# One chip core, three attention-like parts: layer-norm normalisations on ScalarE, and other slots for statistics, projections and fetches

## What is computed

```python
x = x + _layernorm(_L0_attn_ref(_layernorm(x), w_qkv, w_out, b_out))
x = x + _layernorm(_L0_ffn_ref(_layernorm(x), ...))
# _L0_ffn_ref:
for l in range(2):
    x = x + _attn(_ln(x, ln1_w[l], ln1_b[l]), wq[l], wk[l], wv[l], wo[l], ...)   # 16 heads of 8, causal
    h = _ln(x, ln2_w[l], ln2_b[l])
    moe = _token_moe if l % 2 == 0 else _seq_moe     # top 2 of 8 experts, per token / per sequence
    x = x + moe(h, ...)                              # experts 128 -> 512 -> 128, exact gelu
# _ln and _layernorm: (x - mean) / sqrt(var + 1e-5), the first with weight and bias
```

## Time and profile of the kernel before

| | |
|---|---|
| Median of 3 runs | 1273.79 us (1273.51 to 1277.96) |
| The profiled execution | 1271.35 us, of which the trace spans 1269.6 |
| Mean granted clock of TensorE | 0.943 |
| TensorE busy | 1064.3 us (84%) |
| VectorE busy | 936.9 us (74%) |
| ScalarE busy | 767.8 us (60%) |
| GpSimd busy | 663.6 us (52%) |

### The profile page before, as it was taken

How to read it: one execution, slowest core, us unless ns; L and a number is a source line. 1 busy time by engine, 2 the same in 40 slices (tenths; PEclk the granted TensorE clock), 3 DMA queues, 4 the chain that set the end, 5 groups by cost and what they waited for, 6 DMA issues and landing times. The chain is left out here.

```text
span 1269.6 us, 36493 instructions
## 1 busy us (share of the span) xinstructions
PE 1064.3 (84%) x10172; PEld 795.5 (63%) x10267; DVE 936.9 (74%) x2774; ACT 767.8 (60%) x1745; POOL 663.6 (52%) x986
## 2 busy tenths in 40 slices
PE   1888999999999899998199997387888989959997
PEld 0565666666666666665199997255655656638996
DVE  3678999999988889997523332278889888865665
ACT  1566777777777777776066564156657667645554
POOL 3345565566556777776611111566676666422332
PEclk8899999999999999999599999589989899988999
DMA  5332111111112122211222222243221211100000
GB/s 148 93 96 78 51 49 38 42 49 52 53 52 59 45 64 63 67 51 37 75 63 70 70 70 71 56 115 103 76 65 39 65 47 55 53 2 9 17 21 21
DMA packets 120793, 74.57 MB, mean 59 GB/s; under 512 B 7936, under 2 KB 115712, under 8 KB 120704
## 3 DMA queue, kind: packets, MB, share of 16 engines
q1 hardware_dynamic: 101536, 54.48, 15.5%
q10 hardware_dynamic: 15072, 10.61, 2.9%
q0 software_dynamic: 4096, 8.40, 2.2%
HBM read 22.21 MB, written 12.71 MB: 28 GB/s over the span
## 5 line engine op out<-in xcount | busy, mean ns | idle before, releaser
L608 DVE TENSOR_REDUCE negm<-bank 128x2 f32<-128x512 f32 (+1 forms) x576 | 389.1, 679 | 84.2 <-PE bank L300 59.0
L496 ACT ACTIVATE prob<-bank 128x512 f32<-128x512 f32 x576 | 339.7, 595 | 126.6 <-PE bank L322 88.5
L889 POOL TENSOR_SCALAR_AFFINE_SELECT prob<-prob 128x512 f32<-128x512 f32 x384 | 248.3, 648 | 171.3 <-ACT prob L496 169.1
L341 PE MATMUL bank<-prob,vaug 128*32 128x256 f32 (+1 forms) x3072 | 168.7, 338 | 1.6 <-POOL prob L889 1.3
L308 PE MATMUL bank<-stack 126*128 126x256 bf16 x768 | 152.3, 280 | 0.0
L327 PE MATMUL bank<-stack 128*128 128x256 bf16 x768 | 150.7, 278 | 0.9 <-ACT prob L496 0.9
L1180 POOL COPY w_job<-w_s 128x512 f32 x72 | 47.1, 655 | 191.7 <-PE bank L1150 183.0
L1161 PEld LDWEIGHTS bank<-w_job,prob 128*128 128x128 f32 x1152 | 139.6, 192 | 3.6
L1161 PE MATMUL bank<-w_job,prob 128*128 128x128 f32 x1152 | 139.9, 275 | 0.0
L341 PEld LDWEIGHTS bank<-prob,vaug 128*32 128x32 f32 x3072 | 81.6, 111 | 78.5 <-issue 46.7
L1172 ACT ACTIVATE prob<-bank,b_job 128x256 f32<-128x256 f32 x288 | 118.2, 469 | 16.4 <-PE bank L1150 15.1
(11 more groups left out here) (180 smaller groups left out, 2003.7 us busy)
## 6 DMA issues: line engine op xcount, KB each, us to landing
stack<-parts SPq DMA_DIRECT2D x288, 128.0 KB
w_s<-e_w ACTq DMA_DIRECT2D x32, 256.0 KB, 2.9
oT<-x_routed SPq DMA_DIRECT2D x40, 128.0 KB, 2.1
y_routed<-oT SPq DMA_DIRECT2D x40, 128.0 KB, 1.8
stack<-mT SPq DMA_DIRECT2D x192, 4.0 KB
out<-x_all SPq DMA_DIRECT2D x16, 128.0 KB, 1.8
b_all<-e_b ACTq DMA_DIRECT2D x2, 512.0 KB, 8.3
x_routed<-hk,x_at POOLq DMA_INDIRECT x64, 2.3
```

The costliest lines, as they stand in the source:

```text
L341: m = nc.tensor.matmul(o, w, (prob0, prob1)[kb][:, g % 2, h], start=kb == 0, stop=kb == 1, skip_group_check=True)
L496: nc.scalar.activation(o, s, ACT.Exp, scale=SCALE).then_inc(exp_done, 1)
L608: nc.vector.tensor_reduce(o, s, AX.X, ALU.max, negate=True).then_inc(max_done, 1)
L889: nc.gpsimd.affine_select(out=t, in_=t, compare_op=ALU.is_ge, fill=0.0, base=0, pattern=[[0, HG], [1, P]], channel_multiplier=-1).then_inc ...
```

## The change

The normalisation (x - mean) * r is written as x * r + c with c = -mean * r, so that ScalarE's activation can do it with scale and bias by partition. GpSimd computes c for both tiles of an item (`pool_shift`, two small operations) behind each `pool_rstd` of xn and of att/hn, always in slot 2. ScalarE writes xn in slot 3 (`act_xn`, behind the copy mT) and att or hn at the end of slot 2 (`act_post`). The normalisation `f` stays on VectorE.

Moved on VectorE: f from slot 0 to slot 1 (ahead of the reductions of that slot, and one more step behind: item first), the statistics and moments of the new x from slot 3 to slot 0 of the next step, the combine of phase 2 from slots 0 and 1 (item nxt2) to slots 2 and 3 of the step before (nxt3). On TensorE: `pe_o3` from slot 0's end to an early place in slot 1, `pe_v` from the end of slot 2 (item nxt) to the end of slot 1 (item cur, the step after); ScalarE's writes of v go from slot 3 to slot 2. On GpSimd: the power for f from slot 0 to slot 3, the fetches from one per slot to two in slot 3 (item 4 ahead) and two in slot 0 (item 3 ahead), always behind the slot's last select. The run of phase 2 begins one step sooner. The four writes of q and k keep their order: the fourth now stands at the start of slot 1 instead of the end of slot 0. Three semaphores are new (`post_n`, `x_rstd`, `f_ok`); what waited for `res` of the normalisations waits for these.

```diff
-NPRE, NRSTD, NRES, NSPLIT = 4, 4, 14, 3
+NPRE, NRSTD, NRES, NSPLIT = 4, 4, 10, 3
...
-            at = lo - (3 if hi == 3 * B else 2)
+            at = lo - (4 if hi == 3 * B else 2)
...
         def pe_hT(i):
-            pe.wait_ge(res, NRES * i.v + NRES)
+            pe.wait_ge(post_n, 2 * i.v + 2)
...
+            if k == 1 and older:
+                pe_o3(older)
...
             if im:
-                if gm == 0:
+                if gm == 1:
                     pe.wait_ge(v_sb, im.v + 1)
-                if gm == 2 and nxt:
-                    pe.wait_ge(v_sb, nxt.v + 1)
                 pe_max_T(im, gm)
...
-            if k == 0 and older:
-                pe_o3(older)
...
-            if k == 2 and nxt:
-                if im:
-                    pe.wait_ge(mT_sb, 4 * im.v + gm + 1)
-                pe_v(nxt)
+            if k == 1 and cur:
+                pe.wait_ge(mT_sb, 4 * cur.v + 1)
+                pe_v(cur)
...
+        def act_normal(dst, src, r, c, s):
+            for j in range(2):
+                nc.scalar.activation(dst[j], src[j], ACT.Identity, scale=r[:, j:j + 1],
+                                     bias=c[:, j:j + 1]).then_inc(s, 1)
+        def act_xn(i):
+            act.wait_ge(pre_rstd, NRSTD * i.v + NRSTD)
+            need(act, xT_ps, i.v - 1)
+            act_normal([xn[:, i.par, j] for j in range(2)], tiles(x_all if i.phase == 0 else f_all, i),
+                       pre_r[:, i.par], pre_c[:, i.par], xn_ok)
+        def act_post(i):
+            act.wait_ge(post_rstd, NRSTD * i.v + 4)
+            if i.phase == 0:
+                dst = src = [att[:, i.par, j] for j in range(2)]
+            else:
+                dst, src = [hn[:, i.par, j] for j in range(2)], tiles(f_all, i)
+                need(act, hT_ps, i.v - B - 1)
+                if i.phase == 1:
+                    need(act, hk_sb, i.v - B - 1)
+            act_normal(dst, src, post_r[:, i.par], post_c[:, i.par], post_n)
...
         def act_slot(step, k):
-            cur, nxt, nxt2, old, older = (item(step, d) for d in (0, 1, 2, -1, -2))
+            cur, nxt, nxt2, older = (item(step, d) for d in (0, 1, 2, -2))
             (ie, ge), (io, go), (im, gm) = group(step, k, 2), group(step, k, 4), group(step, k, 1)
-            if k == 3 and nxt:
-                act_values(nxt)
+            if k == 1 and nxt:
+                act_qk(nxt, 3)
+            if k == 2 and cur:
+                act_values(cur)
             if io:
                 act_oT(io, go)
             if ie:
                 act_exp(ie, ge, 0)
             if im:
                 act_mT(im, gm)
+            if k == 3 and nxt2:
+                act_xn(nxt2)
             if k == 0 and nxt:
                 act_qk(nxt, 0)
+                act_qk(nxt, 1)
...
+            if k == 2 and older:
+                act_post(older)
             if k == 0 and nxt:
-                act_qk(nxt, 1)
+                act_qk(nxt, 2)
...
-        def dve_normalise(i):
-            dve.wait_ge(post_rstd, NRSTD * i.v + (2 if i.phase == 0 else NRSTD))
-            if i.phase > 0:
-                need(dve, hT_ps, i.v - B - 1)
-                if i.phase == 1:
-                    need(dve, hk_sb, i.v - B - 1)
-                dve_normal([hn[:, i.par, j] for j in range(2)], tiles(f_all, i), post_mv[:, i.par],
-                           post_r[:, i.par], res, NRES - 7)
-            else:
-                att_j = [att[:, i.par, j] for j in range(2)]
-                dve_normal(att_j, att_j, post_mv[:, i.par], post_r[:, i.par], res)
...
         def dve_f(i):
-            dve.wait_ge(post_rstd, NRSTD * i.v + NRSTD)
-            dve_normal(tiles(f_all, i), tiles(x_all, i), mv2[:, i.par], r2[:, i.par], res)
+            dve.wait_ge(x_rstd, 2 * i.v + 2)
+            for j in range(2):
+                nc.vector.tensor_scalar(tiles(f_all, i)[j], tiles(x_all, i)[j], mv2[:, i.par, j, 0:1],
+                                        r2[:, i.par, j:j + 1], ALU.subtract, ALU.mult).then_inc(f_ok, 1)
...
+            if k == 1 and first and first.phase == 0:
+                dve_f(first)
...
-            if k == 3 and nxt2:
-                dve.wait_ge(pre_rstd, 2 * nxt2.v + 2)
-                need(dve, xT_ps, nxt2.v - 1)
-                dve_normal([xn[:, nxt2.par, j] for j in range(2)], tiles(x_all if nxt2.phase == 0 else f_all, nxt2),
-                           pre_mv[:, nxt2.par], pre_r[:, nxt2.par], xn_ok)
...
-            if k == 0 and nxt2 and nxt2.phase == 2:
-                dve_combine(nxt2, 0)
             if k == 0 and oldest and oldest.phase == 0:
-                dve_f(oldest)
+                dve_stats(tiles(x_all, oldest), st2, res, NRES * oldest.v + 6)
...
-            if k == 3 and older and older.phase == 0:
-                dve_stats(tiles(x_all, older), st2, res, NRES * older.v + 8)
+            if k == 3 and nxt3:
+                dve_combine(nxt3, 1)
...
-            if k == 1 and nxt2 and nxt2.phase == 2:
-                dve_combine(nxt2, 1)
-            if k == 2 and older:
-                dve_normalise(older)
+            if k == 0 and oldest and oldest.phase == 0:
+                need(dve, x_rstd, 2 * (oldest.v - 2) + 2)
+                dve_moments(st2, mv2[:, oldest.par], res, NRES * oldest.v + 6)
+            if k == 2 and nxt3:
+                dve_combine(nxt3, 0)
...
-            if k == 3 and older and older.phase == 0:
-                need(dve, post_rstd, NRSTD * (older.v - 2) + 4)
-                dve_moments(st2, mv2[:, older.par], res, NRES * older.v + 8)
...
+        def pool_shift(mv, r, c, s, base, last=1):
+            pool.wait_ge(s, base)
+            alone(pool)
+            for j in range(2):
+                nc.gpsimd.tensor_scalar(c[:, j:j + 1], mv[:, j, 0:1], r[:, j:j + 1], -1.0, ALU.mult,
+                                        ALU.mult).then_inc(s, last if j else 1)
...
-                pool_rstd(post_mv[:, older.par], post_r[:, older.par], post_rstd, NRSTD * older.v,
-                          1 if older.phase == 0 else NRSTD - 1)
-            if k == 0 and oldest and oldest.phase == 0:
-                pool.wait_ge(res, NRES * oldest.v + 12)
-                pool_rstd(mv2[:, oldest.par], r2[:, oldest.par], post_rstd, NRSTD * oldest.v + 2)
+                need(pool, post_n, 2 * (older.v - 2) + 2)
+                pool_rstd(post_mv[:, older.par], post_r[:, older.par], post_rstd, NRSTD * older.v)
+                pool_shift(post_mv[:, older.par], post_r[:, older.par], post_c[:, older.par], post_rstd,
+                           NRSTD * older.v + 2)
...
             if ie:
                 pool_select(ie, ge, 0)
+            if k == 3 and oldest and oldest.phase == 0:
+                pool.wait_ge(res, NRES * oldest.v + NRES)
+                need(pool, f_ok, 2 * (oldest.v - 2) + 2)
+                pool_rstd(mv2[:, oldest.par], r2[:, oldest.par], x_rstd, 2 * oldest.v)
...
-                pool_rstd(pre_mv[:, nxt2.par], pre_r[:, nxt2.par], pre_rstd, 2 * nxt2.v)
+                pool_rstd(pre_mv[:, nxt2.par], pre_r[:, nxt2.par], pre_rstd, NRSTD * nxt2.v)
+                pool_shift(pre_mv[:, nxt2.par], pre_r[:, nxt2.par], pre_c[:, nxt2.par], pre_rstd,
+                           NRSTD * nxt2.v + 2)
...
-            nxt3 = item(step, 3) if step_phase(step) == 2 else None
-            if nxt3:
-                pool_fetch(nxt3, k)
+            if step_phase(step) == 2 and k in (0, 3):
+                fetched_item = item(step, 4 if k == 3 else 3)
+                for n in range(2):
+                    if fetched_item:
+                        pool_fetch(fetched_item, n if k == 3 else 2 + n)
```

More of the change, by code:

```diff
@@ L102, in build @@
         pre_r = sb("pre_r", [P, 2, 2])
+        pre_c = sb("pre_c", [P, 2, 2])
         xn = sb("xn", [P, 2, 2, P])
@@ L507, in act_mT, with act_qk @@
             nc.scalar.copy(mT[:, g % 2], mid_bank[0:2 * HG, 0:P].bitcast(BF16)).then_inc(mT_sb, 1)
-        def act_qk(i, t):
-            if t == 0:
+        def act_qk(i, n):
+            t = n // 2
+            if n == 0:
                 act.wait_ge(qk_ps, i.v + 1)
@@ L514, in act_qk @@
                 need(act, stack_dma[i.par], stack_ready(i) - 16 * STACK_DMAS)
-            for o in (qkf[:, t], parts[:, i.par, t, 0]):
-                nc.scalar.activation(o, pre_bank[:, t * T:(t + 1) * T], ACT.Identity,
-                                     bias=bqk_s[:, i.phase, t:t + 1]).then_inc(qkf_sb, 1)
+            o = parts[:, i.par, t, 0] if n % 2 else qkf[:, t]
+            nc.scalar.activation(o, pre_bank[:, t * T:(t + 1) * T], ACT.Identity,
+                                 bias=bqk_s[:, i.phase, t:t + 1]).then_inc(qkf_sb, 1)
         def act_values(i):
@@ L636, in dve_stats, with dve_moments @@
                 nc.vector.bn_stats(st[:, j], src[j]).then_inc(s, 1)
-        def dve_moments(st, mv, s, base):
+        def dve_moments(st, mv, s, base, last=1):
             dve.wait_ge(s, base + 2)
@@ L642, in dve_moments @@
             for j in range(2):
```

(9 more changed lines are left out.)

16 lines of the change are left out of this document (9 added, 7 removed).

## The result

The changed kernel takes 1293.7 us (median; 1289.04 to 1296.28), the kernel before 1273.88 (1273.51 to 1277.96). The ratio is 1.0144, with a 95% interval of 1.0108 to 1.018: slower by about 20 us. The forecast was 1276.2, with 1263 to 1290.

A forecast was written before the change was run, and what follows sets the result against it. The prediction took the chain from GpSimd's `rest` through the DMAs to bound each step, not VectorE. Its terms, -2.3 + 0 + 2.6 + 0.5 + 2.6 - 1.8 + 0.8 = +2.4 us, gave 1276.2 us, range 1263 to 1290.

The forecast's parts named there:

- the rival of 1222 us: VectorE is the bound, so each of 45 steps loses 1.2 us: -54 us; chance 0.06.
- the rule "until `rest` starts plus 11.9": Every step lasts the time until GpSimd's `rest` starts plus 11.9 us, through casts and DMAs to the next step.
- act_post ahead of `oT`: Slot 2 on ScalarE: `oT` 0.4 us late, nearly all covered by TensorE's waits; 0 a step (-0.1 to +0.35).
- GpSimd's four small operations: Slot 2 on GpSimd: 1 us more a step, covered save for act_post, since the selects are wanted a slot later.
- Phase 1: Slot 3 on ScalarE: the xn pair ahead of hT costs 0.2 us a step (0 to 0.4), x13 = +2.6.
- The emptying of the pipeline: Last items of phases 1 and 2: ScalarE's pairs and the shifts show, +0.5 and +0.8 us.
- Phase 2, start, first fetches: Kernel start -2.3 us; first fetches of phase 2 +2.6; phase 2 steps 19.45 to 19.5, together -1.8.
- one slow step in nine: Phase 2: the slow clock comes in one step of nine, adding 0.2 us to the mean step.
- The +2.6 for the start of phase 2: Item 1's fetches ahead of item 0's work, 1.6 us not hidden, with shift and ScalarE's pair +2.6 (1 to 3).
- 0.1 a step at most: Slot 2, L352 (L355 after the change) waiting for ScalarE's write of v: nothing, or 0.1 us at most.
- Projections: TensorE: v and o3 moved fill the wait at L352, but TensorE then waits at L322 for `mT`: nothing.
- The rival that came true: ScalarE's queue stands behind GpSimd's shift, `oT` 1.1 us late, 0.4 in all 42 middle steps: 1290; chance 0.26.

The follow-up runs named there:

- e9: e5 with GpSimd's shift left out and ScalarE given r as bias, so the mean is not taken off; 1272.9 us, ratio 0.9997 to the kernel before.
- e6: Changed kernel with both normalisations (xn, att/hn) back on VectorE and no shift on GpSimd; 1265.6 us, ratio 0.9941 to the kernel before.
- e1: Changed kernel with act_post moved from the end of slot 2 to slot 3, right behind the copy oT; 1291.3 us, ratio 1.0147 to the kernel before.
- e13: e6 with GpSimd computing both shifts in slot 2 all the same, read by nobody; 1278.1 us, ratio 1.0044 to the kernel before.
- e11: e6 with the projections v and o3 back in slots 2 and 0; 1266.9 us, ratio 0.9943 to the kernel before.
- e10: e6 with an idle pair of ScalarE activations added at the end of slot 2, output unused; 1266.6 us, ratio 0.9946 to the kernel before.
- e5: Changed kernel with xn's normalisation back on VectorE and its shift removed, att/hn still on ScalarE; 1289.3 us, ratio 1.0133 to the kernel before.

## Why the prediction was wrong, step by step

*What bounds the kernel.* Right in that VectorE does not: its relief was worth nothing (e9 against e6), and the rival of 1222 us is far off. Right too that TensorE's own path is nearly as long as the DMAs' chain. But the rule "until `rest` starts plus 11.9" did not hold in phase 0: `rest` to the next step is 280.45 - 268.17 = 12.28 there, since TensorE's own path now ended the step. In phase 2 it is 974.63 - 962.97 = 11.66. I went on as if the DMAs had a margin to give, from the one row of 0.35 and the other of 0.22. Over the stretch the waits of L300 for DMAs are 1.6 us in ten steps of the kernel before, 0.16 a step.

*act_post ahead of `oT`: the term that failed.* The time of `oT` was right: 13.5 to 13.6 us into the step by my sum, measured 13.49. That is partly luck, since two errors cancel: the shift with its wait took 0.71 and not 0.5, and the power came 0.06 later and not 0.25. My "0.4 late" also left out the 0.13 us from the end of `oT` to L389. The mis-sized term is what TensorE had to give. L389 ran 0.55 later than before, and only 3.88 - 3.71 = 0.17 came back between it and the next step (273.21 to 277.09, 276.74 to 280.45). I took nearly all of the 0.4 as covered and put 0 a step into the sum; 0.38 a step is left here, 6.7 us in phase 0 together with its first steps.

*GpSimd's four small operations: covered, I wrote, save for act_post.* They were not. The selects are wanted in the slot after, but there was no half microsecond left in it: L344 waits 5.3 us in eight steps of e1 and 7.8 in ten of e13. I had read GpSimd's share of busy time, 100.66 of 171 us, and not the arrival of the select that ends last.

*Phase 1.* +0.2 a step was expected from xn ahead of hT. L363 does wait for hT, 1.8 us in eight steps, but the wait for `oT` is there again, 4.0 us in nine steps, which I had taken as 0; L325's grew from 3.9 to 7.6 us in the same stretch. Measured +0.65 a step.

*The emptying of the pipeline: +0.5 and +0.8 forecast, +3.4 and +5.3 measured.* There nothing hides the chain. The last `oT` of phase 1 stands behind act_post, and this behind the shift:

```profile
616.04 0.88 ACT L555 ACTIVATE hn<-f_all,post_c,post_r 128x128 f32<-128x128 f32 x2 [3.87 <-POOL post_c L897]
616.82 0.35 ACT L502 COPY oT<-bank 128x256 f32<-128x256 f32 x1
...
617.51 1.09 PE L389 MATMUL bank<-ident,oT 128*128 128x128 f32 x4 [3.53 <-ACT oT L502]
```

The last matmul L344 that `oT` copies from ended at 613.99, so `oT` stood 2.8 us behind act_post. I had costed the length of the added operations and not what is queued behind the one that waits. In e1, with act_post behind `oT`, the two stretches take 61.55 and 41.16 us in place of 63.30 and 44.53 (59.95 and 39.24 before).

*Phase 2, start, first fetches: right in the numbers, in phase 2 by luck.* `rest` starts 962.97 - 955.60 = 7.37 us into a step (forecast 7.3), the step is 19.03 (19.2), the mean 19.33 (19.45), the granted clock falls to 0.50 in four early steps and in none after, in place of six all along, L691 took 0.42 in place of the held 1.89, and the start gained 2.2. But the mean comes out by two errors that cancel: from item 33 to 37 the four steps with the fall take 20.16 to 20.54 us, where I had one slow step in nine, and the eight behind them 18.9 on average, 0.3 under the 19.2. The +2.6 for the start of phase 2 is also less than its named parts (1.6 + 0.5 + 0.875) without a reason given; measured +1.6. And L355 waits 14.3 us in eleven steps for ScalarE's write of v, which stands behind the cast of the later `rest`; I had 0.1 a step at most. As I read it this only moves a wait from L325: e11, with the projections back, has no shorter phase 2 step than e6 (19.35 and 19.15).

*Projections.* "Nothing", by my reading. In phase 0, e11 to e6, it is 0.11 a step; in sum it depends on the other parts. *The rival that came true* is the slower one, ScalarE's queue behind GpSimd's shift, at 1290 and with a chance of 0.26. Its deciding point, 0.3 us of lateness, was set too high: the margin was 0.17. The numbers for it lay in my own sum. That its total is near is in part luck: it has 0.4 us in each of 42 steps, where phase 2 got shorter and the two emptyings cost 8.6 us; and it has only one of the shift's two ways.

## What to carry to other kernels

Before an instruction that waits is put into an in-order queue, ask what stands behind it and when that is wanted; the instruction's own length may be free (e10) while the wait ahead of it is not (16.4 us from e9 to e5). Where a normalisation is rewritten for another engine, the extra small operations (here the shift) count on the engine that computes them too, and busy shares do not show it: look at the arrival of the last select or copy against the matmul that takes it. A margin should be summed over a stretch of steps, not read from the largest wait of one.

## What the runs showed of the hardware

Two GpSimd operations on a 128x1 column each took 0.50 us together, with 0.21 ahead of them for the result of the power: 0.71 for 256 numbers, as long as the power itself (0.71). The two activations on ScalarE took 0.88 in steady steps while GpSimd and VectorE were busy, and 0.875 in the tail; each single one of this form in the changed kernel took 477 to 495 ns. This agrees with the Trainium skill, "SBUF — State Buffer", section "Who interferes with whom", by which ScalarE is not held by the other two. VectorE's pair for f, now next to `rest`, took 1.26 us in the step shown (against 0.6 that I assumed). One of its instructions took 332 to 705 ns in the changed kernel, median 668, and 335 to 344 in the kernel before, where f stood in another slot.
